# The third stage of a fused transformer decoder block: its fp32 products as three products of rounded parts, one input loaded transposed, mask rows sent with the fills

## The chip, the cores and the metric

The kernel runs as one program on 1 core of one Trainium2 chip. The metric is device time of the whole program in microseconds (us). Three runs of the kernel before gave 4870.12, 4870.19 and 4873.30 us, median 4870.19 us.

## The reference, cut to what matters

Input `x` is 128 x 128 x 256 (batch, channel, length), `ctx` has the same shape. Four stages follow each other:

```
x1  = LN(attn_conv(q=x, k=v=ctx, causal mask) + x)          # 8 heads, grouped conv of width 3 as projection
o1  = LN(x1 + mha1(x1, x1, x1, mask1))                      # 16 heads of depth 16, d_model 256
o2  = LN(o1 + mha2(v=ctx, k=ctx, q=o1, mask2 per batch))    # queries from o1, keys and values from ctx
out = LN(o2 + relu(o2 @ w1 + b1) @ w2 + b2)

def _mha(v, k, q, mask, wq, bq, wk, bk, wv, bv, wo, bo):
    qh = split(q @ wq + bq); kh = split(k @ wk + bk); vh = split(v @ wv + bv)
    logits = einsum('bhqd,bhkd->bhqk', qh, kh) / sqrt(16) + mask * -1e9
    return einsum('bhqk,bhkd->bhqd', softmax(logits), vh) @ wo + bo
```

The change is about the third stage (`mha2`).

## The kernel before, in words

`build` runs `constants`, then `attention` three times (`phase` 0, 1, 2), then `feed_forward`. A pass of `attention` works on units of 512 tokens; phases 1 and 2 have 32 units of 4 tiles of 128 tokens. The text calls phase 2 the third stage and phase 1 the second.

A unit has 16 slots. `PLANS[phase]` says by hand in which slot each engine does which step, and each engine's program is written out from it (`body(t)`); nothing is scheduled at run time, so a late step holds up all that stands behind it on its engine. Attention of unit t takes slots 0 to 15: in each slot `attend_step` (scores, turned, with the row maxima subtracted) on TensorE, `exp_step` on ScalarE, and after every fourth one `pv_tile` (probabilities times values). In the same slots other units are at other steps: the projections of unit t+2 (`project_step`), the values of unit t+1, the scores of unit t+1 that only serve the row maxima (`score_step`, with `max_of` on VectorE), the output product, residual, moments and normalisation of the tiles just attended.

Where the operands come from matters here. Queries and keys are split into three bf16 parts (`HI`, `MID`, `LO`), and SyncE's queue then copies them with 12 DMAs per half unit (`fill_stack`) into `stack`, from which scores are made: 96 rows of parts, 3 rows of the mask of the batch (`mask_parts`) and 3 rows of maxima. The SP queue has one order: in each unit `fill_mask(t+1)`, `fill_stack(t+1, 1)`, `load(t+3)`, `store(t-1)`, `load_resid(t+1)`, `fill_stack(t+2, 0)`. `fill_mask` therefore stands behind the 12 DMAs of `fill_stack(.., 0)`. The first score of unit t+1 (slot 4) waits for it.

In the third stage all products with weights are plain fp32 products. `ctx` arrives with tokens on partitions, so `context_step` turns it on TensorE (2 steps of 4 transposes a unit) and `context_out` copies it to `cin` on ScalarE. The second stage does the same products in another way: operands are split into two rounded parts of type F32R and multiplied three times (`PRODUCTS`: high x high, high x low, low x high). There ScalarE rounds the input (`round_x`), and GpSimd takes the rest (`rest_of_x`).

Of the kernel before, what the change touches and what calls it, by code (L numbers as in the profile page):

```python
# [22 lines left out]
F32 = mybir.dt.float32  # L23
# [73 lines left out]
        dve_steps={'recip': (5, 2), 'merge': (6, 0), 'add': (8, 1), 'stats': (8, 2), 'moments': (8, 2), 'epsilon': (8, 2)},  # L97
        pe_masks=(),
        split_lag=0,
        work=[((0,), 'context', 2, 0),  # L100
              ((0, 1), 'values', 1, 0),
              ((3,), 'values', 1, 1),
              ((3,), 'turn_y', -1, 2),
              ((5,), 'max', 0, 1),
              ((5, 6), 'project', 2, 0),
              ((7,), 'project', 2, 1),
              ((7,), 'context', 2, 1),
              ((9,), 'project', 2, 2),
              ((10,), 'turn_y', -1, 3),
              ((11,), 'project', 2, 3),  # L110
              ((12,), 'max', 1, 0),
              ((14,), 'turn_y', 0, 0),
              ((15,), 'turn_y', 0, 1)],
    ),
# [118 lines left out]
def constants(nc, top, l0, io, c):  # L233

    def sb(name, shape, dt=F32):
        c[name] = top.enter_context(nc.sbuf_tensor(name, shape, dt))
        return c[name]

    def sb_l0(name, shape, dt=F32):
# [10 lines left out]
    mask1 = sb("mask1", [P, P])  # L250
    mask1t = sb("mask1t", [P, P])
    rows = {n: sb(n, [P, L]) for n in ("ln1_g", "ln1_b", "ln2_g", "ln2_b", "ln3_g", "ln3_b",
                                       "mha1_bo", "mha2_bo", "ffn_b2")}
# [7 lines left out]
    c["weights"] = {m: {n: sb(f"{m}_{n}", [P, 2, L]) for n in ("wq", "wk", "wv", "wo")} for m in ("mha1", "mha2")}  # L261
    c["weights_in"] = top.enter_context(nc.semaphore("weights_in"))
# [133 lines left out]
def attention(nc, top, c, io, phase):  # L396
# [32 lines left out]
    with ExitStack() as ctx:  # L429
# [10 lines left out]
        if conv:  # L440
            x_pad = sb("x_pad", [P, 2, BU, L + 2])
            c_pad = sb("c_pad", [P, 2, BU, L + 2])
        else:
            xin = sb("xin", [P, 2, 2, TOK])
        if phase == 2:
            craw = sb("craw", [P, 2, TILES, L])
            cin = sb("cin", [P, 2, 2, TOK])
        if phase == 0:
            x_parts = [sb(f"{n}_parts", [P, 2, 2, BU, L + 2], F32R) for n in ("x", "c")]
        elif phase == 1:  # L450
            x_rounded = sb("x_rounded", [P, 2, 2, TOK], F32R)
        if not conv:
            wq, wk, wv, wo = (c["weights"][name][n] for n in ("wq", "wk", "wv", "wo"))

        w_split = [] if phase == 2 else [(w, sb(f"w{n}_parts", [P, 2, w.shape[1], w.shape[2]], F32R))
# [1071 lines left out]
```

## Time and profile before

| | |
|---|---|
| median of three runs | 4870.19 us |
| the profiled execution, its own time | 4873.18 us |
| its span (first to last instruction) | 4871.4 us |
| mean granted TensorE clock | 0.970 |
| busy over the span: PE, DVE, ACT, POOL | 90%, 72%, 64%, 58% |
| first and last load of the residual in the third stage | at 2955.9 and 4071.9 us |

PE is TensorE, PEld its weight loads, DVE VectorE, ACT ScalarE, POOL GpSimd, SP the queue of SyncE. Busy shares over the span are means over four stages. What a change in one stage is worth has to be read from the rows of that stage. All times of rows are us from the start of the span, unless ns is written.

### The profile page before, as it was taken

To read this page: it belongs to the slowest core of one execution; us is meant where nothing else is said; L and a number is where in the kernel's file an instruction comes from. 1 tells how busy PE (TensorE), PEld (TensorE's weight loads), DVE (VectorE), ACT (ScalarE), POOL (GpSimd) and SP (SyncE) were. 2 spreads that over 40 slices of the span, in tenths; PEclk is the share of its full clock that TensorE was granted. 3 is DMA by queue.
4 is the path that set the end of the run, shared out by engine and by line. 5 is a ranking of instruction groups with operands and counts; after the bars stand their busy time and mean duration, and the time that the engine had idled before them with its cause. 6 is when DMAs were issued, how large, how long until landed. Compare 5 with 4: busy or idle time off the path is not lost. (4 is left out here: it accounts for less than half of the span.)

```text
span 4871.4 us, 150045 instructions
## 1 busy us (share of the span) xinstructions
PE 4403.9 (90%) x46221; PEld 3437.6 (71%) x46221; DVE 3528.8 (72%) x14161; ACT 3110.8 (64%) x6280; POOL 2832.4 (58%) x4362
## 2 busy tenths in 40 slices
PE   5999999999999958999999967899999996999999
PEld 4777677677777647777777755666666664899998
DVE  4888888888888848888888864555555554666665
ACT  3777777777777747777777754566566664544443
POOL 2655655655656536777777744556565563455555
PEclk8999999999999979999999988999999998999999
DMA  4333333333333325555555534555555553222221
GB/s 100 114 112 113 109 113 109 111 114 108 111 116 107 106 75 157 155 158 165 152 155 164 153 101 140 157 169 162 164 164 162 167 166 111 74 65 77 65 69 56
DMA packets 1047398, 602.17 MB, mean 124 GB/s; under 512 B 64057, under 2 KB 1047017, under 8 KB 1047273
## 3 DMA queue, kind: packets, MB, share of 16 engines
q1 hardware_dynamic: 1037288, 595.97, 42.7%
q10 hardware_dynamic: 9984, 4.72, 0.3%
q8 instruction: 56, 0.92, 0.1%
q14 instruction: 70, 0.57, 0.0%
HBM read 175.86 MB, written 117.54 MB: 60 GB/s over the span
## 5 line engine op out<-in xcount | busy, mean ns | idle before, releaser
L1049 DVE CUSTOM_DVE_ANT_0 l_junk<-l_bank,mask 128x256 bf16<-128x256 f32 x2048 | 775.9, 419 | 126.5 <-PE l_bank L782 104.6
L940 ACT ACTIVATE mha_probs<-mha_bank 128x512 f32<-128x512 f32 x1024 | 607.8, 601 | 330.2 <-PE mha_bank L812 179.7
L940 ACT ACTIVATE l_probs<-l_bank 128x512 f32<-128x512 f32 x1024 | 612.1, 598 | 232.5 <-DVE l_bank L1064 170.7
L1064 DVE TENSOR_TENSOR l_bank<-l_bank,mask0t 128x512 f32<-128x512 f32 x640 | 445.4, 696 | 103.1 <-PE l_bank L812 92.2
L1049 DVE CUSTOM_DVE_ANT_0 mha_junk<-mha_bank,mask 128x128 bf16<-128x128 f32 x2048 | 466.4, 284 | 64.7 <-PE mha_bank L782 61.1
L1040 DVE TENSOR_REDUCE mha_max_parts<-mha_bank 128x4 f32<-128x512 f32 x512 | 331.4, 683 | 217.6 <-PE mha_bank L782 214.2
L782 PE MATMUL mha_bank<-mha_stack 96*128 96x128 bf16 (+1 forms) x4096 | 363.7, 222 | 121.2 <-DMA mha_stack<-mask_parts 41.0
L812 PE MATMUL mha_bank<-mha_stack 99*128 99x128 bf16 (+1 forms) x4096 | 407.5, 222 | 55.9 <-DMA mha_stack<-mha_max_rows 52.2
L782 PE MATMUL l_bank<-l_stack 96*128 96x256 bf16 x2048 | 369.4, 276 | 71.6 <-DVE l_max_parts L1049 56.6
L812 PEld LDWEIGHTS mha_bank<-mha_stack 99*128 99x128 bf16 (+1 forms) x4096 | 305.5, 99 | 174.0 <-issue 54.9
L812 PE MATMUL l_bank<-l_stack 99*128 99x128 bf16 x4096 | 405.1, 221 | 13.6 <-issue 5.3
L1169 POOL TENSOR_TENSOR mha_yproj<-mha_yproj,mha_parts 128x512 f32<-128x512 f32 x256 | 296.7, 1159 | 200.9 <-ACT mha_parts L913 200.8
L1366 ACT ACTIVATE ffn_hidden<-ffn_h,ffn_b_s 128x512 f32<-128x512 f32 x256 | 176.8, 691 | 354.8 <-PE ffn_h L1320 336.4
L812 PEld LDWEIGHTS l_bank<-l_stack 99*128 99x128 bf16 x4096 | 256.1, 99 | 207.0 <-issue 177.7
L1064 DVE TENSOR_TENSOR mha_bank<-mha_bank,mask1t 128x512 f32<-128x512 f32 x512 | 354.8, 693 | 59.9 <-PE mha_bank L812 57.9
L1320 PE MATMUL ffn_h<-ffn_x_parts,ffn_w_parts 128*128 128x512 f32 x1536 | 373.8, 393 | 21.4 <-DVE ffn_x_parts L1381 20.8
L1333 PEld LDWEIGHTS ffn_o<-ffn_w_parts,ffn_hidden_parts 128*128 128x128 f32 x3072 | 384.9, 191 | 11.6 <-issue 2.0
L1333 PE MATMUL ffn_o<-ffn_w_parts,ffn_hidden_parts 128*128 128x256 f32 x3072 | 388.2, 283 | 1.6 <-DVE ffn_hidden_parts L1386 1.6
L782 PEld LDWEIGHTS mha_bank<-mha_stack 96*128 96x128 bf16 (+1 forms) x4096 | 253.6, 98 | 185.6 <-issue 99.6
L1386 DVE TENSOR_TENSOR ffn_hidden_parts<-ffn_hidden,ffn_hidden_parts 128x512 fp32r<-128x512 f32 x256 | 246.4, 963 | 181.5 <-ACT ffn_hidden_parts L1366 180.4
L1320 PEld LDWEIGHTS ffn_h<-ffn_x_parts,ffn_w_parts 128*128 128x128 f32 x1536 | 281.7, 189 | 75.6 <-issue 21.1
L1175 POOL TENSOR_TENSOR mha_parts<-mha_yproj,mha_parts 128x512 bf16<-128x512 f32 x256 | 296.7, 1159 | 59.3 <-ACT mha_parts L977 56.4
(176 smaller groups left out, 11473.5 us busy)
## 6 DMA issues: line engine op xcount, KB each, us to landing
mha_stack<-mha_parts SPq DMA_DIRECT2D x1536, 128.0 KB, 2.4
l_stack<-l_parts SPq DMA_DIRECT2D x1024, 64.0 KB, 2.0
l_stack<-l_parts SPq DMA_DIRECT2D x256, 128.0 KB, 2.3
rows_o<-mha_y SPq DMA_DIRECT2D x64, 512.0 KB, 3.8
cols_o<-mha_y_t SPq DMA_DIRECT2D x128, 256.0 KB, 2.8
l_x_pad<-in_x SPq DMA_DIRECT2D x64, 256.0 KB, 2.8
l_c_pad<-in_ctx SPq DMA_DIRECT2D x64, 256.0 KB, 3.0
l_resid<-in_x SPq DMA_DIRECT2D x64, 256.0 KB, 2.7
```

What stands on the lines that cost most here:

```text
L782: mm = nc.tensor.matmul(sbank[i % 2][:, s * KEYS:(s + 1) * KEYS], stack[0:SCORED, u.par, place(0, h), j * P:(j + 1) * P], stack[0:SCORED, ...
L812: mm = nc.tensor.matmul(tbank[i % 2][:, s * P:(s + 1) * P], stack[0:STACKED, u.par, place(1, h), key:key + P], stack[0:STACKED, u.par, pla ...
L940: nc.scalar.activation(probs[:, i % RING, :], tbank[i % 2][:, :], ACT.Exp).then_inc(att_exp, 1)
L1040: nc.vector.tensor_reduce(max_parts[:, j, 0, col:col + SH * GROUPS - 1:GROUPS], sbank[i % 2][:, :].rearrange("p (s k) -> p s k", s=SH), op ...
L1049: ins = nc.vector.tensor_tensor_reduce(out=junk[:, i % 2, cols], in0=sbank[i % 2][:, cols], in1=mask, scale=1.0, scalar=LOWEST, op0=ALU.ad ...
L1064: nc.vector.tensor_tensor(bank_, bank_, mask.unsqueeze(1).to_broadcast([P, 4, P]), ALU.add).then_inc(att_masked, 1)
L1169: nc.gpsimd.tensor_tensor(rest, rest, parts[:, u.par, i, HI, :], ALU.subtract).then_inc(rest_step, 1)
L1175: nc.gpsimd.tensor_tensor(parts[:, u.par, i, LO, :], rest, parts[:, u.par, i, MID, :], ALU.subtract).then_inc(split_done, 1)
L1320: mm = nc.tensor.matmul(hbank[f % 4][:, :], w1_parts[:, a, kt, f * P:(f + 1) * P], x_parts[:, u.par, b, kt, :], start=(i == 0), stop=(i == 5))
L1333: mm = nc.tensor.matmul(obank[j][:, 0:L], hidden_parts[:, u.par, b, f, j * P:(j + 1) * P], w2_parts[:, a, f, :], start=(f == 0 and i == 0) ...
L1366: last = nc.scalar.activation(out, hbank[f % 4][:, :], ACT.Relu, bias=c["ffn_b1_s"][:, f:f + 1])
L1386: nc.vector.tensor_tensor(hidden_parts[:, u.par, 1, f, :], hidden[:, f % 2, :], hidden_parts[:, u.par, 0, f, :], ALU.subtract).then_inc(h_ ...
```

## The change: what it does

Third stage:

- `ctx` is also given transposed (`ctx_t`), and is loaded by two DMAs of 256 KB straight into `cin`, as `xin` is. `context_step`, `context_out` and the buffer `craw` are gone.
- `xin` and `cin` have one buffer each in place of two. `load(u)` waits until both were split for the unit before (`x_lo`, `c_lo`).
- All products with weights become three F32R products. For that ScalarE rounds `xin` and `cin` (`round_x`, two instructions of 128x1024, in slot 13, for unit t+3), GpSimd takes the rest of `xin` (`rest_of_x`), VectorE the rest of `cin` (`rest_of_c`, new). `merged_out` writes a rounded `merged_t`, and VectorE takes its rest (`merged_low`, new, four a unit). The weights are split at the head of the stage.
- The mask rows go in two halves, each in `fill_stack` ahead of the wait for `split_done`.
- The plan has new slots.

Other stages: the weights of `mha1` are loaded at the head of the first stage and split there, those of `mha2` in the next units; `y` of the third stage lies in the buffer of its raw weights (`carried`). Loops of the first two stages and of the feed-forward are as they were.

```diff
-        score=[4, 4, 6, 7, 8, 8, 9, 9, 11, 11, 12, 12, 13, 14, 15, 17],
+        score=[4, 5, 7, 7, 8, 9, 9, 10, 11, 12, 12, 14, 16, 16, 18, 19],
-        steps={'turn': 6, 'turn_merged': 7, 'output': 8, 'normalise': 9},
+        steps={'turn': 5, 'turn_merged': 7, 'output': 8, 'normalise': 9},
...
+        split_slot=13,
...
             def load(u):
-                if exists(u.plus(-2), N):
+                if phase == 2:
+                    wait_sp(sp, x_lo, u.u, passed["sp"])
+                    wait_sp(sp, c_lo, u.u, passed["sp"])
+                elif exists(u.plus(-2), N):
...
-            def fill_mask(u):
-                wait_sp(sp, att_mm, CHUNKS * (u.u - 1) if u.number() not in (0, 1) else 0, passed["sp"])
-                sp.dma_start(stack[STACK:SCORED, u.par, side_of((1,)), :],
-                             mask2_units[u.u].unsqueeze(1).to_broadcast([3, H, TOK])).then_inc(mask_in[u.par], 16)
...
+                if phase == 2:
+                    sp.dma_start(stack[STACK:SCORED, u.par, side_of((1,)), tokens],
+                                 mask2_units[u.u][:, tokens].unsqueeze(1).to_broadcast([3, H, 2 * P])
+                                 ).then_inc(stack_in[u.par][half], 16)
                 wait_sp(sp, split_done, projected(u, HALVES - 1), passed["sp"])
...
             def output_step(u, j):
+                if phase == 2:
+                    pe.wait_ge(mt_low, TILES * u.u + j + 1)
+                    for kt in range(2):
+                        for a, b in PRODUCTS:
+                            mm = nc.tensor.matmul(fbank[:, 0:L], merged_t_parts[:, b, kt, :], w_parts[3][:, a, kt, :],
...
+            def rest_of_c(u):
+                dve.wait_ge(x_hi, u.u + 1)
+                nc.vector.tensor_tensor(x_part(1, u.par, 1), raw(1, u.par), x_part(1, u.par, 0), ALU.subtract
+                                        ).then_inc(c_lo, 1)
+
+            def merged_low(u, j):
+                dve.wait_ge(mt_out, TILES * u.u + j + 1)
+                nc.vector.tensor_tensor(merged_t_parts[:, 1, :, :], fbank[:, 0:2 * P].rearrange("p (a s) -> p a s", a=2),
+                                        merged_t_parts[:, 0, :, :], ALU.subtract).then_inc(mt_low, 1)
...
+                        if slot == SPLIT_SLOT and exists(t.plus(3), N):
+                            rest_of_c(t.plus(3))
```

How the instructions stand now, at three places. First TensorE in the third stage, where one unit ends and the next begins. `mha_craw` is `ctx` as loaded, `mha_z` the sum to be normalised, `mha_probs` the probabilities. Before:

```order
L860 MATMUL mha_bank<-ident,mha_z 128x128 x2
L848 MATMUL mha_bank<-ident,mha_merged 128x128 x2
L799 ISA
L812 MATMUL mha_bank<-mha_stack 128x128 x4
L822 REGISTER_ALU
L826 MATMUL mha_bank<-mha_probs,mha_vals 17x128 x16
L145 REGISTER_ALU
L716 MATMUL mha_bank<-ident,mha_craw 128x128 x4
L145 REGISTER_ALU
L765 MATMUL mha_bank<-mha_wv,mha_cin 128x256 x2
L854 MATMUL mha_bank<-mha_wo,mha_merged_t 128x256 x2
```

The same place now; L868 was L860, L849 L848, L813 L812, L827 L826, L783 is the score product (L782), and L857 the output product (L854).

```order
L868 MATMUL mha_bank<-ident,mha_z 128x128 x2
L849 MATMUL mha_bank<-ident,mha_merged 128x128 x2
L800 ISA
L813 MATMUL mha_bank<-mha_stack 128x128 x4
L823 REGISTER_ALU
L827 MATMUL mha_bank<-mha_probs,mha_vals 17x128 x16
L144 REGISTER_ALU
L783 MATMUL mha_bank<-mha_stack 128x128 x4
L144 REGISTER_ALU
L783 MATMUL mha_bank<-mha_stack 128x128 x4
L857 MATMUL mha_bank<-mha_w_parts,mha_merged_t_parts 128x256 x6
```

The four transposes of `ctx` are gone, the values have moved behind this place, two score steps have come in, and the output product has 6 instructions in place of 2.

Second, ScalarE in slots 12 to 14 of the third stage, now (L943 is the exponential, L931 and L933 the row maxima and their DMA, L978 `round_x`):

```order
L948 ACTIVATE mha_heads_out<-mha_bank 128x512
L940 REGISTER_ALU
L943 ACTIVATE mha_probs<-mha_bank 128x512
L1009 REGISTER_ALU
L931 ACTIVATE mha_max_rows<-mha_bank 48x256
L933 DMA mha_stack<-mha_max_rows 3x16x256
L972 ISA
L978 ACTIVATE mha_x_pair<-mha_xin 128x1024
L978 ACTIVATE mha_c_pair<-mha_cin 128x1024
L940 REGISTER_ALU
L943 ACTIVATE mha_probs<-mha_bank 128x512
```

Before, the same stretch (with the maxima a slot earlier) had nothing between the DMA and the next exponential:

```order
L945 ACTIVATE mha_heads_out<-mha_bank 128x512
L1003 REGISTER_ALU
L928 ACTIVATE mha_max_rows<-mha_bank 48x256
L930 DMA mha_stack<-mha_max_rows 3x16x256
L937 REGISTER_ALU
L940 ACTIVATE mha_probs<-mha_bank 128x512
L937 REGISTER_ALU
L940 ACTIVATE mha_probs<-mha_bank 128x512
```

Two instructions of 128x1024 have come between two exponentials.

Third, the SP queue at the head of the third stage's loop. Before, where `fill_mask` is L638 and `fill_stack` L656:

```order
L163 ISA
L638 ISA
L638 DMA mha_stack<-mask_parts 3x16x512
L150 ISA x2
L656 DMA mha_stack<-mha_parts 16x16x256 x12
L150 ISA
L621 ISA
L621 DMA mha_xin<-cols_o 128x4x128
```

And now, up to the second input:

```order
L673 ISA
L673 DMA mha_stack<-mask_parts 3x16x256
L149 ISA
L678 DMA mha_stack<-mha_parts 16x16x256 x12
L149 ISA
L646 ISA
L646 DMA mha_xin<-cols_o 128x4x128
L646 ISA
L646 DMA mha_xin<-cols_o 128x4x128
L646 DMA mha_cin<-in_ctx_t 128x4x128 x2
```

What stands here is the second half of a unit's fills, with the second half of its mask; the first half of the mask now stands in the same way ahead of the other 12, at the end of the body of the unit before.

## Rows read from the trace of the kernel before

**Rows 1.** Windows: 25 units of the third stage (busy us by engine).
```profile
3076.00:3968.40 892.40, 815.98 (x8704) 609.55 (x8700) 512.59 (x1201) 551.08 (x1151) 513.97 (x626) 0.98 0.58 164
```

**Rows 2.** Source L646, a move for each of 26 loads: durations, first and last start.
```profile
L646 SPq MOVE mha_resid<-rows_x x26: 29/29/29, 1919.2 to 2757.6; - x26
L646 SPq MOVE mha_resid<-rows_o x26: 29/38/38, 3076.0 to 3968.5; - x26
```

**Rows 3.** Waits in 3076.0 to 3968.4 us: us in total, times, longest.
```profile
PE mha_bank L782 <- DMA mha_stack<-mask_parts: 34.8, 21, 2.8
```

**Rows 4.** Timeline of PE in the third stage: start us, us, engine, line.
```profile
3410.03 1.95 PE L765 MATMUL mha_bank<-mha_wv,mha_cin 128*128 128x256 f32 x8
3411.81 0.38 PE L860 MATMUL mha_bank<-ident,mha_z 128*128 128x128 f32 x2
...
3415.42 0.62 PE L782 MATMUL mha_bank<-mha_stack 99*128 99x128 bf16 x8 [1.79 <-DMA mha_stack<-mask_parts]
...
3422.13 1.94 PE L742 MATMUL mha_bank<-mha_xin,mha_wq 128*128 128x512 f32 x4
3423.91 0.60 PE L716 MATMUL mha_bank<-ident,mha_craw 128*128 128x128 f32 x4
3424.34 0.38 PE L848 MATMUL mha_bank<-ident,mha_merged 128*128 128x128 f32 x2
...
3426.34 1.08 PE L854 MATMUL mha_bank<-mha_wo,mha_merged_t 128*128 128x256 f32 x4
3427.26 0.39 PE L812 MATMUL mha_bank<-mha_stack 102*128 102x128 bf16 x4
...
3429.78 0.39 PE L812 MATMUL mha_bank<-mha_stack 102*128 102x128 bf16 x4
3430.00 0.39 PE L860 MATMUL mha_bank<-ident,mha_z 128*128 128x128 f32 x2
3430.23 0.60 PE L839 MATMUL mha_bank<-ident,mha_heads_out 128*128 128x128 f32 x4
3430.66 0.39 PE L812 MATMUL mha_bank<-mha_stack 102*128 102x128 bf16 x4
```

**Rows 5.** Timeline of PE in the second stage: one value tile, then one projection.
```profile
2708.23 0.39 PE L759 MATMUL mha_bank<-mha_w_parts,mha_x_rounded 128*128 128x256 f32 x1
...
2709.05 0.40 PE L812 MATMUL mha_bank<-mha_stack 99*128 99x128 bf16 x4
...
2711.15 0.47 PE L739 MATMUL mha_bank<-mha_x_rounded,mha_w_parts 128*128 128x512 f32 x1
...
2712.59 0.38 PE L860 MATMUL mha_bank<-ident,mha_z 128*128 128x128 f32 x2
```

**Rows 6.** Timeline of the SP queue in the third stage.
```profile
3403.11 7.91 SPq L656 DMA_DIRECT2D mha_stack<-mha_parts  x12
3411.95 0.29 SPq L638 DMA_DIRECT2D mha_stack<-mask_parts  x1
```

**Rows 7.** Windows: the stretch behind the wait at 3415 us.
```profile
3417.20:3419.80 2.60, 2.60 (x9) 1.17 (x8) 1.24 (x5) 0.86 (x2) 0.55 (x1) 0.51 0.72 200
```

**Rows 8.** Timeline of ACT in the third stage.
```profile
3435.99 0.38 ACT L928 ACTIVATE mha_max_rows<-mha_bank 48x256 bf16<-48x256 bf16 x1
3436.40 0.73 ACTq L930 DMA_DIRECT2D mha_stack<-mha_max_rows  x1
3437.25 1.09 ACT L940 ACTIVATE mha_probs<-mha_bank 128x512 f32<-128x512 f32 x2 [0.88 <-PE mha_bank L812]
```

**Rows 9.** Sources L972 and L1381: ns min/median/max, first and last start us.
```profile
L972 ACT ACTIVATE mha_x_rounded<-mha_xin x32: 1041/1077/1081, 1773.2 to 2797.0; 128x1024 fp32r<-128x1024 f32 x32
L1381 DVE TENSOR_TENSOR ffn_x_parts<-ffn_xin,ffn_x_parts x32: 1217/1219/3442, 4138.3 to 4811.0; 128x1024 fp32r<-128x1024 f32 x32
```

**Rows 10.** Timelines of POOL and DVE in the feed-forward stage.
```profile
4307.45 2.41 POOL L1444 TENSOR_TENSOR ffn_resid<-ffn_resid,ffn_b 128x1024 f32<-128x1024 f32 x1
4307.98 2.43 DVE L1386 TENSOR_TENSOR ffn_hidden_parts<-ffn_hidden,ffn_hidden_parts 128x512 fp32r<-128x512 f32 x1 [2.12 <-ACT ffn_hidden_parts L1366]
```

More of the change, by code:

```diff
@@ L462, in x_part @@
                 return x_parts[n][:, par, part, :, :]
-            return xin[:, par, :, :].bitcast(F32R) if part else x_rounded[:, par, :, :]
+            if phase == 1:
+                return xin[:, par, :, :].bitcast(F32R) if part else x_rounded[:, par, :, :]
+            return c_pair[:, par, part, :, :] if n else x_pair[:, part, :, :]
         resid = sb("resid", [P, 2, TILES * W])
@@ L495, in attention @@
         resid_ld = [sem(f"resid_ld{i}") for i in range(2)]
-        mask_in = [sem(f"mask_in{i}") for i in range(2)]
         padded = sem("padded")
@@ L542, in attention @@
                   if not (conv and pair[0] == pair[1])]
+        FILLED = len(FILLS) + (1 if phase == 2 else 0)
         def place(side, h):
@@ L676, in body @@
             def body(t):
-                if phase == 2 and exists(t.plus(1), N):
-                    fill_mask(t.plus(1))
                 if exists(t.plus(1), N):
@@ L880, in body @@
                             value_step(u, step, bank_, piece, pieces)
-                        elif what == "context":
-                            context_step(u, step, bank_)
                         elif what == "max":
@@ L968, in round_x @@
                     act.wait_ge(xin_ld[u.par], 16 * XIN_LOADS * (u.k + 1))
-                if exists(u.plus(-2), N):
-                    act.wait_ge(work_mm, work_count(u.plus(-2), "values", VSTEPS - 1))
-                for n, x in enumerate(raw):
-                    last = nc.scalar.activation(x_part(n, u.par, 0), x[:, u.par, :, :], ACT.Copy)
+                readers = [(u.plus(-1), "project", GROUPS - 1)] if phase == 2 and exists(u.plus(-1), N) else []
+                readers += [(u.plus(-2), "values", VSTEPS - 1)] if exists(u.plus(-2), N) else []
+                if readers:
+                    act.wait_ge(work_mm, work_count(*max(readers, key=lambda at: banks.at[at[1:]][0])))
+                for n in range(INPUTS):
+                    last = nc.scalar.activation(x_part(n, u.par, 0), raw(n, u.par), ACT.Copy)
                 last.then_inc(x_hi, 1)
@@ L1138, in body @@
                             mid_part(t.plus(2), P_SLOT.index(slot - 1))
-            iterations(nc, dve, N, 2, 1, body)
+                        if slot == SPLIT_SLOT and exists(t.plus(3), N):
+                            rest_of_c(t.plus(3))
+                if conv and t.number() == -1:
+                    for n, parts_ in enumerate(c["mha1_parts"]):
+                        dve.wait_ge(c["next_w_hi"], n + 1)
+                        nc.vector.tensor_tensor(parts_[:, 1, :, :], c["weights"]["mha1"][n], parts_[:, 0, :, :],
+                                                ALU.subtract).then_inc(c["next_w_lo"], 1)
+            iterations(nc, dve, N, 3 if phase == 2 else 2, 1, body)
         @block.gpsimd
@@ L1230, in body @@
                         pad_edges(t.plus(3))
-                    if slot == SPLIT_SLOT and phase != 2 and exists(t.plus(3), N):
+                    if slot == SPLIT_SLOT and exists(t.plus(3), N):
                         rest_of_x(t.plus(3))
```

207 lines of the change are left out of this document (104 added, 103 removed).

## The prediction

> **What bounds the kernel now.** I first took the period of a unit in each stage. Loads of the residual come once a unit, and 26 of them span 892.4 us in the third stage, so a unit takes 35.70 us there; in the second stage it takes 838.4 / 25 = 33.54 us [rows 2]. That is odd, since the second stage does the same products and more work on VectorE. Then I read the windows of the third stage: TensorE is busy 815.98 of 892.4 us (91%), ScalarE 62%, VectorE and GpSimd 57 and 58% [rows 1]. TensorE bounds the stage, with 76.4 us idle, 3.06 us a unit. Of these the mask rows take 34.8 us, 1.39 us a unit [rows 3]. The SP queue shows why: the mask's DMA is issued at 3411.95, behind 12 fills that began at 3403.11, and TensorE stands until 3415.42 [rows 4, 6]. The other 1.67 us a unit are small waits. Behind the long wait the granted clock is 0.51 for a while, which is the lower level (1.2 GHz) [rows 7]; over the stage it is 0.98 [rows 1].
>
> **The work of TensorE, step by step.** Products of fp32 are priced from the third stage, products of rounded parts from the second, start to next start, all at the full clock.
> - Projections, 4 steps a unit. Now 3422.13 to 3423.91 = 1.78 us [rows 4]; as six F32R products 2711.15 to 2712.59 = 1.44 us [rows 5]. Saved 4 x 0.34 = 1.36.
> - Values, 4 tiles a unit. Two tiles now take 3410.03 to 3411.81 = 1.78, one 0.89 [rows 4]; as six products 2708.23 to 2709.05 = 0.82 [rows 5]. Saved 4 x 0.07 = 0.28.
> - Output product, 4 a unit. Now 3426.34 to 3427.26 = 0.92 [rows 4]; afterwards six products of the very shape of a value tile, 0.82. Saved 4 x 0.10 = 0.40.
> - Transposes of `ctx`, 2 steps a unit: 3423.91 to 3424.34 = 0.43 each [rows 4]. Saved 0.86.
>
> Together 2.90 us a unit, for 32 units 93 us. All of it lies on the engine that bounds the stage. I see no reason why it should be less than zero or more than 3.3 (the same with 0.05 more for each of the eight 256-column tiles).
>
> **The waits of TensorE.** The mask's 1.39 us go: its halves are now issued before the wait for the last split, well ahead of the fills. What is late next at slot 4 is the 12 fills themselves. The mask was issued at 3411.95 and released TensorE at 3415.42, 3.5 us later; the last of the 12 fills was issued at about 3410.4 (one takes 7.91 / 12 = 0.66), so by the same delay it was there at about 3413.9. TensorE arrived at 3415.42 - 1.79 = 3413.6 [rows 4, 6]. So fills and TensorE arrive together today, and a TensorE that does the same slots 1.6 us sooner (context, two output products, the values and a part of the waits) would wait up to 1.9 us for fills. That would eat the gain from the mask, unless something else holds TensorE up between slot 12 and slot 4. Something does:
>
> ScalarE gets two rounding instructions of 128x1024 in slot 13. One takes 1.04 us [rows 9]. In the order they stand behind the row maxima and their DMA, ahead of exponential 14, and TensorE may not start chunk 0 of the next unit before exponential 14 is done. From the end of chunk 13 on TensorE: exponential 13 about 0.65 with its start, maxima 0.41 (3435.99 to 3436.40), DMA issue 0.85 (to 3437.25) [rows 8], two roundings 2.08 [rows 9], exponential 14 about 0.5 (two take 1.09 [rows 8]). Sum 4.49. TensorE itself has there: maxima turned and `turn_heads` 0.22 + 0.43, chunk and score 14 0.22 + 0.23, chunk 15 0.22, two `turn_y` and one `turn_merged` 3 x 0.22, together 1.98 (each from the four rows from 3429.78 on and from 3424.34 [rows 4]; I take 0.22 for all 2-matmul steps). New wait: 2.5 us. Then values of chunk 15 wait for exponential 15, about 0.2. ScalarE's `context_out` is gone, but in slots where it wasn't on this path; it counts as nothing.
>
> VectorE gets `rest_of_c`, again 128x1024: alone 1.22 us [rows 9]. It starts when the rounding ends, so it ends 0.6 us after exponential 14 if undisturbed, and score 13 and the output product of tile 2 need the maximum and `merged_low` behind it. Undisturbed this adds nothing. But GpSimd's rest of `xin` and its affine steps read SBUF at the same time. In the feed-forward stage such a subtraction of half the size took 2.43 us, ending 0.55 us after a GpSimd addition of 2.41 us that had begun 0.53 us before it [rows 10]: it did nothing until GpSimd was through. So `rest_of_c` costs 1.22 us at best, and 2.41 + 1.22 = 3.6 at worst for one collision. I take 1.9, nearer to the lower end: in my chain GpSimd is in the second affine instruction of tile 1 when `rest_of_c` becomes ready, the long rest of `xin` stands behind that, and in rows 10 VectorE got its turn as soon as one GpSimd instruction ended. This adds 0.5 us to the wait at the output product. `merged_low` (four a unit, reads PSUM and one operand in SBUF) lies beside a `pv_tile` and costs nothing; if VectorE is late, it carries the delay over, which is counted.
>
> The Trainium skill (SBUF — State Buffer, Who interferes with whom) states the rule behind this: a VectorE instruction with two SBUF inputs and a GpSimd instruction that reads SBUF exclude each other, whichever starts first keeps the port pair to its end. By that rule, the two rests, both released by the same rounding, cannot overlap at all; the row agrees (2.43 us). It is what the second rival is made of.
>
> New waits: 2.5 + 0.2 + 0.5 = 3.2 us a unit, where there were 3.06. With TensorE 3.2 us late in slot 0 it is no longer early at slot 4, so the fills cost nothing. The other waits of 1.67 us I count as gone: two of them sat between slots 13 and 15, inside the stretch that ScalarE now sets. Bounds: 0.5 (ScalarE ready sooner, as there is slack of one exponential) plus 1.9 for the fills, against 5.7 if `rest_of_c` takes 3.6. Net I take +0.14 a unit, +4 us in 32 units. The clock: a stretch with 3.2 us of waits is as likely to be followed by the low level as the present one; I keep 0.98 and count nothing. Bound: 2% of 35.7 is 0.7 us a unit if it never falls.
>
> **Loads.** With one buffer, `load(t+3)` is issued after both sets of 12 fills: from the first fill 2 x 8.2 (7.91 and a mask of 0.29 [rows 6]), then four issues of about 0.5, so 18.4 us, and needs some 3 us to land. The rounding is a unit later, 31 us after the first fill. Hidden with 9 us to spare.
>
> **The ends.** At the head of the third stage ScalarE rounds four weights (each 512 columns, half of 1.04, so 2.1 us together, beside the input's DMA), then both inputs 2.1, then GpSimd 2.4 [rows 9, 10] before the first projection, which before waited for DMAs alone. That is about +3 us. In the first stage four more DMA issues stand between the first fills, and three weights are split in line ahead of unit 0: +3 us. The second stage starts without splitting, but its first product waits for the input's split anyway: 0. Together +6 us, between 0 and +12.
>
> **Sum.** -93 + 4 + 6 = -83 us against the profiled execution's own 4873.18 us (span 4871.4), so 4790. That execution is 3.0 us above the median, so against the median of 4870.19 it gives 4787 us. I correct nothing else. The unit comes out at 35.70 - 2.90 + 0.14 = 32.9 us.
>
> **Rivals.** All are for the median.
> 1. *The waits dissolve.* ScalarE runs ahead enough for the two roundings, because exponential 13 and the maxima come sooner than in my chain; then the fills set slot 4, at 1.9 us a unit, and the clock falls less (0.5 us a unit gained). Unit: 35.70 - 2.90 - 3.06 + 1.9 + 0.5 of other waits - 0.5 = 31.6; -130 + 6: 4746 us. For it: VectorE and GpSimd have over 40% idle, ScalarE 38% [rows 1]. Against: ScalarE is strictly in order there.
> 2. *The lock, once.* The rest of `xin` starts first on GpSimd, and `rest_of_c` takes 3.6 us, not 1.9: +1.7 a unit, 54 us, 4841 us. For it: both are released by the same rounding. Against: GpSimd is in its affine steps when that comes.
> 3. *Slower: the lock, twice.* GpSimd goes from the rest of `xin` straight on to the bias of the residual, also 128x1024 (2.41 us [rows 10]), without VectorE getting in. `rest_of_c` then ends 2.4 us later still, score 13, the output product and the normalisation behind it too: +2.4 x 32 = 77 on the second rival, 4918 us. The place is VectorE in slots 14 to 0; it decides once `rest_of_c` ends more than 2.6 us a unit later than forecast (83 / 32). Against: in rows 10 VectorE gets the port as soon as one GpSimd instruction ends.
> 4. *It is no faster product for product*: the six products change the loaded operand more often, and only the transposes are gained: -28 (32 x 0.86) + 4 + 6, 4852 us. Against: rows 5 are just these products in such company.
>
> **How the numbers follow.** Forecast (4770 to 4810) 0.50; first rival 0.24; second 0.13; third 0.06; fourth 0.07. A measurement of this kernel can tell 0.2% (10 us) from no change, thus 4860 and 4880 are the borders. Faster: all of the forecast and first rival, 0.11 of the second, 0.04 of the fourth, 0.89. Same: 0.02 + 0.03 = 0.05. Slower 0.06. The range leaves out the lower third of the first rival (0.08) and the third, with parts of the second and fourth above it: 4728 to 4852.
>
> **What the changed profile would show.** Right: a period of 32 to 33.5 us between residual loads in the third stage; no wait of the score product for `mask_parts`; a wait of TensorE's chunk 0 for `mha_probs` of ScalarE of about 2 us a unit, with `round_x` running ahead of it; projection steps of 1.44 us there; `rest_of_c` between 1.2 and 2.5 us in the mean. First rival: waits for DMA `mha_stack<-mha_parts` at the first score and a period under 32. Second and third: `rest_of_c` at 3.6 us or more and a score product or output product that waits for VectorE. My chain would be wrong if TensorE's waits lie in other slots than 13 to 0, for there I found none.

## The result, and the profile after

The kernel after took 4720.83 us (median of four runs, 4716.57 to 4722.3); beside it the kernel before took 4871.74 us (4870.12 to 4883.3). The ratio is 0.9684, 95% interval 0.9667 to 0.9701: 3.2% faster. I had forecast 4787 us in a range of 4728 to 4852. The direction was right, the gain was nearly twice the forecast, and the time lies just below the range. The profiled execution took 4722.3 us (span 4720.5 us), 150.9 us less than the profiled one before.

The windows view of the third stage after, for 25 units again (columns as in [rows 1]: stretch, its length, busy us of PE, PEld, DVE, ACT and POOL, granted clock, DMA share, GB/s), and the source of the residual's load, that gives the period:

```profile
3065.40:3832.10 766.70, 714.62 (x9083) 609.68 (x9072) 610.66 (x1323) 577.16 (x1147) 596.35 (x648) 1.00 0.66 191
```

```profile
L664 SPq DMA_DIRECT2D mha_resid<-rows_o x32: 394/507/1135, 2966.4 to 3928.1; - x32
L664 SPq MOVE mha_resid<-rows_x x26: 29/34/38, 1923.7 to 2762.4; - x26
L664 SPq MOVE mha_resid<-rows_o x26: 29/29/29, 3065.4 to 3832.2; - x26
```

A unit takes (3832.2 - 3065.4) / 25 = 30.67 us in place of 35.70 [rows 1, 2], 5.03 us less. The second stage stands where it stood: 838.7 / 25 = 33.55 us. TensorE's idle time is (766.7 - 714.6) / 25 = 2.08 us a unit in place of 3.06, and the granted clock 1.00 in place of 0.98 [rows 1]. The 150.9 us come from three places: from the first to the last load of the stage it is 961.7 us in place of 1116.0 (-154.3); the first load comes 10.5 us later, at 2966.4; and from the last load to the end it is 7.1 us less.

The waits of TensorE in that window (waited for, us in total, times, longest):

```profile
PE mha_bank L868 <- DVE mha_z L1095: 37.4, 25, 1.5
PE mha_bank L840 <- DVE mha_z L1124: 6.7, 25, 0.3
PE mha_bank L813 <- ACT mha_probs L943: 6.4, 24, 0.3
```

The mask is gone from the list [rows 3], and so is every DMA: the fills didn't take its place. What is left sits between chunk 13 of one unit and chunk 0 of the next (chunk n is the attention step of slot n), as forecast, but the greater part stands under the normalised `z`, which `turn_y` (L868) turns; L840 is `turn_heads`. TensorE's timeline there (start us, us, engine, line; idle before it in brackets):

```profile
3376.43 0.40 PE L813 MATMUL mha_bank<-mha_stack 102*128 102x128 bf16 x4
...
3377.34 0.63 PE L840 MATMUL mha_bank<-ident,mha_heads_out 128*128 128x128 f32 x4 [0.29 <-DVE mha_z L1124]
...
3378.48 0.39 PE L868 MATMUL mha_bank<-ident,mha_z 128*128 128x128 f32 x2
3380.36 0.41 PE L868 MATMUL mha_bank<-ident,mha_z 128*128 128x128 f32 x2 [1.50 <-DVE mha_z L1095]
3380.61 0.38 PE L849 MATMUL mha_bank<-ident,mha_merged 128*128 128x128 f32 x2
3381.28 0.38 PE L813 MATMUL mha_bank<-mha_stack 102*128 102x128 bf16 x4 [0.29 <-ACT mha_probs L943]
...
3390.36 0.40 PE L783 MATMUL mha_bank<-mha_stack 99*128 99x128 bf16 x4
...
3390.91 0.96 PE L857 MATMUL mha_bank<-mha_w_parts,mha_merged_t_parts 128*128 128x256 f32 x6
3391.72 0.40 PE L813 MATMUL mha_bank<-mha_stack 102*128 102x128 bf16 x4
...
3395.01 1.62 PE L750 MATMUL mha_bank<-mha_x_pair,mha_w_parts 128*128 128x512 f32 x6
3396.46 0.38 PE L849 MATMUL mha_bank<-ident,mha_merged 128*128 128x128 f32 x2
```

The fp32 rows of [rows 4] have these for an answer: a projection is 3396.46 - 3395.01 = 1.45 us (forecast 1.44), an output product 3391.72 - 3390.91 = 0.81 (forecast 0.82). L783 is the score product of slot 4, the first that needs the fills. The queue of SyncE issued them here:

```profile
3380.16 7.91 SPq L678 DMA_DIRECT2D mha_stack<-mha_parts  x12
```

The last of the 12 was issued at about 3387.4 (3380.16 + 11 x 0.66), and the score product began 3.0 us later without a wait.

ScalarE's timeline beside it shows the chain I had worked out, in its order: exponential 13, maxima, their DMA, two roundings, exponentials 14 and 15.

```profile
3376.86 0.60 ACT L943 ACTIVATE mha_probs<-mha_bank 128x512 f32<-128x512 f32 x1 [0.45 <-PE mha_bank L813]
3377.36 0.36 ACT L931 ACTIVATE mha_max_rows<-mha_bank 48x256 bf16<-48x256 bf16 x1
3377.75 0.73 ACTq L933 DMA_DIRECT2D mha_stack<-mha_max_rows  x1
3378.64 1.06 ACT L978 ACTIVATE mha_x_pair<-mha_xin 128x1024 fp32r<-128x1024 f32 x1 [0.93 <-ACT mha_max_rows L931]
3379.61 1.04 ACT L978 ACTIVATE mha_c_pair<-mha_cin 128x1024 fp32r<-128x1024 f32 x1
3380.55 1.06 ACT L943 ACTIVATE mha_probs<-mha_bank 128x512 f32<-128x512 f32 x2
```

VectorE, then GpSimd, in the same stretch:

```profile
3379.08 1.14 DVE L1095 TENSOR_SCALAR mha_z<-mha_z,mha_moments,mha_rstd 128x256 f32<-128x256 f32 x1
3380.68 1.44 DVE L1041 TENSOR_TENSOR mha_c_pair<-mha_cin,mha_c_pair 128x1024 fp32r<-128x1024 f32 x1 [0.46 <-ACT mha_c_pair L978]
```

```profile
3378.92 1.15 POOL L1202 TENSOR_TENSOR mha_parts<-mha_yproj,mha_parts 128x512 bf16<-128x512 f32 x1
3380.30 0.74 POOL L1236 TENSOR_TENSOR carried<-mha_z,ln_g 128x256 f32<-128x256 f32 x1 [0.23 <-DVE mha_z L1095]
3381.12 1.59 POOL L1238 TENSOR_TENSOR carried<-carried,ln_b 128x256 f32<-128x256 f32 x1
```

The sources of two VectorE lines (ns min/median/max, first and last start):

```profile
L1041 DVE TENSOR_TENSOR mha_c_pair<-mha_cin,mha_c_pair x32: 1220/1404/1670, 2927.1 to 3875.5; 128x1024 fp32r<-128x1024 f32 x32
```

```profile
L1095 DVE TENSOR_SCALAR mha_z<-mha_z,mha_moments,mha_rstd x128: 402/414/1366, 2998.0 to 3967.6; 128x256 f32<-128x256 f32 x128
```

`rest_of_c` takes 1.40 us in the median, not the 1.9 I took, and no score or output product is in the list of waits behind it. It is GpSimd that loses here: its L1238 began 0.44 us after `rest_of_c` and took 1.59 us, where its like (L1236) takes 0.74. One line higher VectorE lost: the normalisation (0.41 us in the median) began 0.16 us after GpSimd's L1202 and took 1.14, to 0.15 us after L1202 had ended. The Trainium skill (SBUF — State Buffer, Who interferes with whom) states both cases: the engine that comes second stands still until the other's instruction is through, and besides a two-input subtraction a `tensor_scalar` can take the shared ports too. By that rule, the trace agrees in both that the second engine is held (1.59 and 1.14 us). By the recorded times it does not show a full standstill: the held instructions ended 0.59 and 0.15 us after the other had ended, less than the 0.74 and 0.41 us that they take alone.

### The profile page after: what moved, and what is told of

It reads as the page before. It is cut to its first block and busy times, and to the rows that moved or that the text cites. A ratio compares the mean times of both kernels' runs of the same rounds, so it can differ in the third digit from the quotient of the medians.

```text
span 4720.5 us, 151301 instructions
## 1 busy us (share of the span) xinstructions
PE 4284.9 (91%) x46733; PEld 3450.4 (73%) x46733; DVE 3659.4 (78%) x14325; ACT 3147.0 (67%) x6284; POOL 2939.8 (62%) x4394
## 5 line engine op out<-in xcount | busy, mean ns | idle before, releaser
L943 ACT ACTIVATE mha_probs<-mha_bank 128x512 f32<-128x512 f32 x1024 | 606.7, 600 | 252.4 <-DVE mha_bank L1084 146.0
L943 ACT ACTIVATE l_probs<-l_bank 128x512 f32<-128x512 f32 x1024 | 611.5, 597 | 234.0 <-DVE l_bank L1084 174.6
L813 PE MATMUL mha_bank<-mha_stack 99*128 99x128 bf16 (+1 forms) x4096 | 407.9, 223 | 61.0 <-DMA mha_stack<-mha_max_rows 53.9
L783 PE MATMUL l_bank<-l_stack 96*128 96x256 bf16 x2048 | 369.4, 276 | 70.7 <-DVE l_max_parts L1069 56.6
L783 PE MATMUL mha_bank<-mha_stack 96*128 96x128 bf16 (+1 forms) x4096 | 370.8, 222 | 54.2 <-DMA mha_stack<-mha_parts 37.0
L813 PE MATMUL l_bank<-l_stack 99*128 99x128 bf16 x4096 | 405.8, 221 | 14.7 <-issue 6.5
L813 PEld LDWEIGHTS l_bank<-l_stack 99*128 99x128 bf16 x4096 | 256.5, 99 | 210.1 <-issue 181.2
L813 PEld LDWEIGHTS mha_bank<-mha_stack 99*128 99x128 bf16 (+1 forms) x4096 | 287.1, 99 | 133.7 <-DMA mha_stack<-mha_max_rows 38.0
L783 PEld LDWEIGHTS mha_bank<-mha_stack 96*128 96x128 bf16 (+1 forms) x4096 | 255.3, 99 | 117.8 <-issue 46.7
L1202 POOL TENSOR_TENSOR mha_parts<-mha_yproj,mha_parts 128x512 bf16<-128x512 f32 x256 | 297.8, 1163 | 58.8 <-ACT mha_parts L983 56.5
```

The costliest lines, as they stand in the source:

```text
L783: mm = nc.tensor.matmul(sbank[i % 2][:, s * KEYS:(s + 1) * KEYS], stack[0:SCORED, u.par, place(0, h), j * P:(j + 1) * P], stack[0:SCORED, ...
L813: mm = nc.tensor.matmul(tbank[i % 2][:, s * P:(s + 1) * P], stack[0:STACKED, u.par, place(1, h), key:key + P], stack[0:STACKED, u.par, pla ...
L943: nc.scalar.activation(probs[:, i % RING, :], tbank[i % 2][:, :], ACT.Exp).then_inc(att_exp, 1)
L1202: nc.gpsimd.tensor_tensor(parts[:, u.par, i, LO, :], rest, parts[:, u.par, i, MID, :], ALU.subtract).then_inc(split_done, 1)
```

## The experiments

After the result, what was open: how much the mask gave by itself; whether the waits of 2.1 us are one chain or two that end together; what the products gave; and where 0.7 us a unit had come from that neither waits nor product durations account for. The last is the clock. Over the 25 units, the stretches at the lower level (1.2 GHz) add up to 44.4 us before and 6.8 us after. My estimate is that a low stretch costs half its length where TensorE has work, by the two levels of 1.2 and 2.4 GHz; so this is worth (44.4 - 6.8) / 25 / 2 = 0.75 us a unit.

For each kernel the same reading was made. "Low" is the time at the lower level, and the last column is the median against the kernel before, measured beside it.

| kernel | unit us | idle us | low us | median us | ratio (95%) |
|---|---|---|---|---|---|
| before | 35.70 | 3.06 | 1.77 | 4871.74 | |
| after | 30.67 | 2.08 | 0.27 | 4720.83 | 0.9684 (0.9667 to 0.9701) |
| after_again | 30.68 | 2.11 | 0.41 | 4720.66 | 0.9682 (0.9666 to 0.9698) |
| a_mask_halves_only | 34.10 | 1.68 | 1.50 | 4824.10 | 0.9887 (0.9871 to 0.9904) |
| b_mask_late | 32.75 | 2.81 | 3.14 | 4792.01 | 0.9828 (0.9807 to 0.9849) |
| c_act_extra | 32.70 | 3.14 | 2.73 | 4778.21 | 0.9791 (0.9774 to 0.9807) |
| d_fp32_output | 32.06 | 2.07 | 2.73 | 4749.63 | 0.9733 (0.9717 to 0.9750) |
| e_turn_y_later | 31.00 | 2.37 | 0.41 | 4732.11 | 0.9703 (0.9687 to 0.9719) |
| f_turn_y_later_round_15 | 31.60 | 2.91 | 0.27 | 4756.00 | 0.9750 (0.9734 to 0.9767) |
| i_slots_of_before | 33.08 | 2.93 | 2.73 | 4788.58 | 0.9818 (0.9802 to 0.9835) |
| k_one_more_transposition | 31.38 | 2.05 | 1.37 | 4740.79 | 0.9716 (0.9699 to 0.9733) |
| l_four_more_transpositions | 31.45 | 1.95 | 0.96 | 4746.44 | 0.9734 (0.9718 to 0.9750) |

The change of idle time and half the change of low time don't always sum to the change of the unit: in the experiments below about 0.3 us a unit can be left, either way. Terms smaller than that are not shown by this count.

**The mask alone, in the kernel before.** Nothing else of the change is in it.

```diff
+                if phase == 2:
+                    sp.dma_start(stack[STACK:SCORED, u.par, side_of((1,)), tokens],
+                                 mask2_units[u.u][:, tokens]...).then_inc(stack_in[u.par][half], 16)
                 wait_sp(sp, split_done, projected(u, HALVES - 1), passed["sp"])
...
-                if phase == 2 and exists(t.plus(1), N):
-                    fill_mask(t.plus(1))
```

> The kernel before with one part of the change: the mask rows in halves, each ahead of its fills. Theory 1 (the wait for the mask and the low clock behind it are a large part of the gain): the wait of 1.4 to 1.5 us a unit goes and slow clock falls from 44 us to under 15 us in 25 units, 0.6 us a unit; 32 x 2.0 = 64 us less, about 4806 us. Rival (as in the prediction: fills arrive with TensorE, and the clock does not depend on this wait): fills take over 0.3 us or more of the wait, the clock stays, 30 to 45 us less, 4825 to 4840 us.

The unit fell by 1.60 us, the time to 0.9887. Its windows and its waits:

```profile
3066.60:3919.10 852.50, 810.48 (x8708) 608.25 (x8704) 512.01 (x1201) 551.45 (x1152) 514.64 (x626) 0.98 0.60 172
```

```profile
PE mha_bank L779 <- DVE mha_max_parts L1037: 19.6, 25, 0.8
PE mha_bank L857 <- DVE mha_z L1072: 19.3, 25, 0.8
PE mha_bank L809 <- issue: 2.7, 12, 0.2
PE mha_bank L779 <- DMA mha_stack<-mha_parts: 0.4, 1, 0.4
```

The wait for the fills is 0.4 us in 25 units. With the mask's 34.8 us away, nothing took their place. The 1.9 us for fills that I had given the first rival doesn't appear.

The time, 55 us less, lies between what the two theories gave (64, and 30 to 45). The clock half of mine failed: low time fell to 37.5 us in 25 units and not to under 15. The clock records show where it went. Of the 13 low stretches before, 7 begin within 2 us behind the end of a wait for the mask, the other 6 at the small waits at the end of a unit. Without the mask's wait all 11 begin there, 6.4 to 7.0 us behind the load of the residual. They come regularly, each 68.2 or 68.3 us after the last, which is two units of 34.10.

**The mask late, in the kernel after.** The whole mask goes back behind 12 fills; all else stays.

```diff
-                if phase == 2:
-                    sp.dma_start(stack[STACK:SCORED, u.par, side_of((1,)), tokens], ...)
...
+                if phase == 2 and exists(t.plus(1), N):
+                    fill_mask(t.plus(1))
```

> The changed kernel with the mask rows as one transfer behind the 12 fills of the first half, as before. Issued at about 3388.4 in the period that was read, it would land 3.5 us later, at 3391.9, where TensorE arrives at 3390.4. Theory 1: 1.5 us a unit of wait and 0.6 us of low clock, +67 us, about 4788 us. Rival (the waits in slots 13 to 0 give the time back, and the clock holds): under +25 us.

```profile
PE mha_bank L874 <- DVE mha_z L1101: 37.5, 25, 1.5
PE mha_bank L789 <- DMA mha_stack<-mask_parts: 20.0, 19, 2.4
PE mha_bank L846 <- DVE mha_z L1130: 6.8, 25, 0.3
PE mha_bank L819 <- ACT mha_probs L949: 4.3, 16, 0.3
```

The wait for the mask came back with 20.0 us, 0.80 us a unit. The unit grew by 2.08: 0.73 of idle and (3.14 - 0.27) / 2 = 1.43 of low clock, which is 0.08 too much. So in the changed kernel the late mask costs more by the clock than by itself. But the low clock doesn't stand behind the mask's wait: of the 23 low stretches 4 begin there, and 19 at the 1.50 us wait for `z`, which the kernel after has as well with 2 low stretches in all. The time came out near the 4788 us that I expected, with half the wait (0.80 for 1.5) and twice the clock (1.43 for 0.6), so the number was luck.

**More work for ScalarE in slot 13.** Ahead of each of the two roundings stands one pass of 128x512 into a buffer that nothing reads. If ScalarE's chain has slack under the wait for `z`, some of it vanishes.

```diff
+                    if phase == 2:
+                        wait(act, extra_done, 2 * u.u + n)
+                        nc.scalar.activation(extra[:, :], raw(n, u.par)[:, 0, :], ACT.Copy).then_inc(extra_done, 1)
```

> The changed kernel with two more instructions of 128x512 on ScalarE among the roundings of slot 13 (0.5 to 0.6 us each, results unused). Theory 2 (ScalarE's in-order chain from exponential 13 to exponential 14 sets chunk 0 of the next unit, with at most 0.3 us of slack): +0.8 to 1.1 us a unit, +26 to 35 us, about 4750 us. Rival (the normalisation on VectorE, held by the port that it shares with GpSimd, sets that stretch, and ScalarE has slack): under +10 us.

```profile
PE mha_bank L870 <- DVE mha_z L1100: 37.5, 25, 1.5
PE mha_bank L815 <- ACT mha_probs L945: 32.5, 25, 1.4
PE mha_bank L842 <- DVE mha_z L1129: 7.0, 25, 0.3
```

The wait for `mha_probs` rose from 6.4 to 32.5 us, 1.04 us a unit, which is what two such passes take (0.52 to 0.53 us each, from start to start). ScalarE's chain has no slack. The low clock took up to 1.23 us a unit on top; with the 1.06 of idle that is 0.26 more than the 2.03 by which the unit grew. I had expected about 4750 us, and the clock is what I had left out.

**The output product as fp32.** `merged_low` and the six products of L857 give way to two fp32 products with a copy of the weights.

```diff
-                        for a, b in PRODUCTS:
-                            mm = nc.tensor.matmul(fbank[:, 0:L], merged_t_parts[:, b, kt, :], w_parts[3][:, a, kt, :], ...
+                for kt in range(2):
+                    mm = nc.tensor.matmul(fbank[:, 0:L], merged_t[:, kt, :], wo[:, kt, :], ...
```

> The changed kernel with the output product of the third stage back in plain fp32 (two products in place of six, no merged_low on VectorE). Theory 3 (the six products are worth their start-to-start difference, 0.92 against 0.80 us, four a unit): +15 us, about 4736 us. Rival (merged_low on a VectorE that is 80% busy costs as much as the products save): within 5 us of 4721 us, or below.

```profile
3061.50:3863.10 801.60, 749.77 (x8876) 624.79 (x8868) 575.94 (x1222) 577.78 (x1147) 594.90 (x648) 0.96 0.64 183
```

The idle time is that of the kernel after (2.07 against 2.08 us), and yet a unit takes 1.39 us more. Four output products, from start to start 0.92 us each and not 0.80, should give 0.48. Low clock gives (2.73 - 0.27) / 2 = 1.23, which leaves 0.16 of the 1.39 for them; so the product step by itself is worth between 0.16 and 0.48 us a unit, and I can't say it closer. I had expected 15 us more, and it is 29. It is the clock that makes this kernel slower, and at the same idle time: it doesn't follow the sum of the waits.

**The second `turn_y` a slot later.** If the wait for `z` alone set the end of the unit, moving its reader behind chunk 0 would save up to 1.5 us a unit. If ScalarE's chain ends at the same time, it saves nothing.

```diff
-        work=[((1, 2), 'values', 1, 0),
+        work=[((0,), 'turn_y', -1, 1),
+              ((1, 2), 'values', 1, 0),
...
-              ((15,), 'turn_y', 0, 1)],
```

> The changed kernel with the turn of tile 1's normalised rows (turn_y) moved from slot 15 to slot 0 of the next unit, so that TensorE does not wait there for VectorE's normalisation (1.50 us a unit). Theory 2 (ScalarE's chain exponential 13, maxima, two roundings, exponential 14 is as late as the normalisation): the wait moves to chunk 0 of the next unit (for mha_probs), the sum of both falls by 0.3 us a unit at most, the time stays within 10 us of the base. Rival (the normalisation alone set it): 1.2 us a unit or more, 38 us less.

```profile
PE mha_bank L813 <- ACT mha_probs L943: 40.0, 25, 1.6
PE mha_bank L849 <- DVE mha_merged L1109: 8.9, 25, 0.4
```

TensorE from chunk 13 to chunk 0 of the next unit:

```profile
3133.83 0.40 PE L813 MATMUL mha_bank<-mha_stack 102*128 102x128 bf16 x4
...
3138.68 0.38 PE L813 MATMUL mha_bank<-mha_stack 102*128 102x128 bf16 x4 [1.63 <-ACT mha_probs L943]
```

The wait for `z` is gone and the wait for `mha_probs` has gone from 6.4 to 40.0 us. From chunk 13 to chunk 0 it is 3138.68 - 3133.83 = 4.85 us, the very time of the kernel after. The unit is 0.33 us longer, and the kernel 11 us slower, where I had expected it within 10. Two chains end together: in the kernel after, ScalarE's was forecast and hidden behind the other one's name in the list.

**That, and the roundings in slot 15.** This takes the roundings out of ScalarE's chain too.

```diff
-        split_slot=13,
+        split_slot=15,
```

> As the kernel before it, and the roundings in slot 15 in place of 13, where TensorE has the product with the values, two scores and an output product ahead of the next exponential that it needs. Theory 2: both chains are gone, 1.5 to 2 us a unit of waits less; then TensorE comes to slot 4 early and waits there for the fills, up to 0.5 us on the trace read (fills at about 3390.3, arrival 3390.4 less 2); net 0 to 1 us a unit, 0 to 30 us less. Rival (GpSimd is then late with the rest of the input, the bias and the reciprocal root of tile 2): new waits of turn_y in slot 3, no gain or a loss of 30 us.

```profile
PE mha_bank L840 <- DVE mha_z L1124: 44.5, 49, 1.6
PE mha_bank L813 <- DMA mha_stack<-mha_max_rows: 14.4, 25, 2.5
PE mha_bank L868 <- DVE mha_z L1095: 4.5, 24, 0.2
```

Both waits went (0.18 us a unit is left of the one for `z`), and others came, so that idle time is 0.8 us more: `turn_heads` for the residual's addition, and chunks for the maxima's DMA. I had named neither of these. The kernel is 35 us slower than the kernel after beside it. Slot 13 is the better of the two places.

**The kernel after again**, as a base for the two experiments before it and the next.

> The changed kernel once more, as the base of this call. 4716 to 4722 us on the chip of the first runs; low clock 0.1 to 0.4 us a unit and a period of 30.67 us if its clock is a trait of the kernel; 1 us of low clock or more and some 30 us more time if it was chance.

4720.66 us against 4720.83, a unit of 30.68 against 30.67 us: even the low clock repeats (0.41 and 0.27, three stretches and two).

**The slots of before, in the kernel after.** The other tables of the plan go back in the same way, and the roundings stay in slot 13.

```diff
-        score=[4, 5, 7, 7, 8, 9, 9, 10, 11, 12, 12, 14, 16, 16, 18, 19],
+        score=[4, 4, 6, 7, 8, 8, 9, 9, 11, 11, 12, 12, 13, 14, 15, 17],
-        steps={'turn': 5, 'turn_merged': 7, 'output': 8, 'normalise': 9},
+        steps={'turn': 6, 'turn_merged': 7, 'output': 8, 'normalise': 9},
```

> The changed kernel with the slots of the plan before (without the two context steps; merged_low in slot 7, roundings in slot 13). Everything else of the change stays. Theory 4 (products, mask and loads carry the gain, the slots little): recorded waits 1.5 to 3 us a unit, +0 to 30 us. Rival (the new slots are what makes room for roundings and merged_low): waits over 3.5 us a unit, +50 us or more.

```profile
3069.50:3896.40 826.90, 753.55 (x9104) 630.19 (x9100) 575.63 (x1324) 578.69 (x1151) 595.75 (x650) 0.96 0.62 178
```

It takes 68 us more than the kernel after beside it, where my theory had 0 to 30. A unit has 2.41 us more: 0.85 of idle, 1.23 of low clock, and about 0.3 that I can't place. The new slots are thus worth nearly half of the whole gain, half of this again by the clock. Taken off one at a time, the early mask (2.08 us a unit) and the slots (2.41) with the products' own time (about 3.0, below) make more than the 5.03 of the whole, so the parts don't add up: the old slots have a price of their own once the roundings stand in slot 13.

**One transposition more, and four.** These ask what brings the low clock back: fp32 output products as in the experiment above, or a longer unit. The line stands in the output step of the third stage, in its first tile alone (`j == 0`), or in all four:

```diff
+                if phase == 2 and j == 0:
+                    for a in range(2):
+                        mm = nc.tensor.transpose(fbank[:, a * P:(a + 1) * P], merged[:, a * P:(a + 1) * P], c["ident"][:, :])
```

> One transposition pair of merged more per unit of the third stage, its result overwritten at once (about 0.22 us of TensorE each time, by the 0.43 us that a group of four such matmuls takes between starts). What is open is what brings the 3.4 us stretches at 1.2 GHz back: d_fp32_output had the same waits as after (2.07 against 2.08 us a unit) and 2.73 us a unit at the low clock against 0.27. Theory A, it follows what TensorE computes at the time (d's four-byte products themselves): the clock here stays as in after (about 0.3 to 0.4 us a unit low), period 30.7 + 0.2 = 30.9 us, time 4720.8 + 25 x 0.22 = 4726 us. Theory B, it follows how long the unit is (d's period of 30.8 before the low clock came on top): some low stretches return here, 1 to 2.7 us a unit, which is 0.5 to 1.2 us of period, time 4740 to 4755 us.

> The same with four pairs per unit, one in each output slot: about 0.88 us of TensorE more per unit and no wait added. Theory A (the clock follows the four-byte products of d): 0.3 to 0.4 us a unit at the low clock, period 30.7 + 0.9 = 31.6 us, time 4721 + 22 = 4743 us. Theory B (it follows the length of a unit): about 2.7 us a unit low, as in d and in the kernels with the slots of before, period 31.6 + 1.2 = 32.8 us, time about 4773 us. Where the added work is partly hidden by the waits of 2.1 us a unit (the wait for the normalisation in the output slot's second product is 1.5 us), the waits fall by what it covers and the period grows by less than 0.9.

Neither theory holds for both. The first run came out as theory B had it (1.37 us low, 4740.79 us). The second is near theory A in time (4746.44 us for 4743), though not in low clock (0.96 us for 0.3 to 0.4). One added pair brought the low time from 0.27 to 1.37 us a unit and lengthened the unit by 0.71 us: 0.55 by the clock, the rest its own work. With the output products as in the kernel after, this isn't a matter of fp32 output products. But four pairs brought less (0.96 us) in a unit of the same length, and the unit of 31.60 us above had 0.27: it isn't the length of a unit either. The windows of the first of the two, in two units on end: for each the stretch of the wait, begun 0.2 us into it, and the stretch behind that:

```profile
3105.20:3108.60 3.40, 1.73 (x36) 1.35 (x40) 2.88 (x4) 3.40 (x7) 3.09 (x3) 1.00 0.24 66
3108.70:3112.00 3.30, 3.30 (x31) 2.81 (x20) 2.22 (x5) 1.79 (x5) 3.30 (x3) 0.50 0.66 183
3137.50:3140.90 3.40, 1.77 (x36) 1.43 (x40) 2.93 (x4) 3.40 (x7) 3.09 (x3) 1.00 0.24 65
3140.90:3144.30 3.40, 3.40 (x47) 3.06 (x40) 3.01 (x9) 2.43 (x6) 3.40 (x3) 1.00 0.71 198
```

The two first stretches are alike in everything, with the same wait:

```profile
3106.52 0.41 PE L871 MATMUL mha_bank<-ident,mha_z 128*128 128x128 f32 x2 [1.50 <-DVE mha_z L1098]
...
3138.82 0.41 PE L871 MATMUL mha_bank<-ident,mha_z 128*128 128x128 f32 x2 [1.50 <-DVE mha_z L1098]
```

Once the clock fell behind it (0.50) and once it didn't (1.00). So what TensorE did in the wait's own stretch doesn't choose the units. The choice is not without order either: in this trace the low stretches of the 25 units, past the first, begin by turns 61.4 and 95.6 us apart (to 0.1 us), two and three units. What makes this order is open; no run varied it by itself.

## Why the prediction was wrong, step by step

**The products** were the soundest term. Forecast 2.90 us a unit; by starts, in medians of the steps at the full clock over 25 units, the projections gave 1.18 (forecast 1.36), the values 0.50 (0.28), the output products 0.45 (0.40), and the transposes of `ctx` 0.87 (0.86): together 3.00. The values have more than I read from single places: a tile after takes 0.76 to 0.81 us (forecast 0.82) for 0.89 to 0.92 before. It is within the bound of 3.3, and 0.10 x 32 = 3 us of the miss. The unit's change less idle and clock, 5.03 - 0.98 - 0.75 = 3.30, leaves 0.3 that I can't place.

**"The waits of TensorE", +0.14 a unit.** This step failed: idle time fell by 0.98. The mask went as said, and alone in the kernel before this gave 1.60 us a unit. The chain on ScalarE was right to within 0.2: from chunk 13 (3376.43) to chunk 0 (3381.28) are 4.85 us, forecast 4.49 and a start of 0.22. What failed is how its price was entered. First, 2.5 and 0.2 us are losses from start to start. The measured loss by the same count is 4.85 - 0.22 - 1.98 = 2.65, but I set it against 3.06 us of recorded idle. As recorded idle it is 2.08 (1.50 + 0.29 + 0.29 in the timeline), since the recorded end of a matmul lies behind the point at which the next could begin: the two of 3380.61 take 0.22 us to the next start elsewhere, but end on record at 3380.99, and idle time counts from there. The two readings differ by about 0.5 us a unit, and one stood on each side of my subtraction. Second, 0.5 us for `rest_of_c` behind GpSimd was wrong: it took 1.40 us, and GpSimd stood back. The two make 1.1 us a unit, some 36 us over 32 units, which is this step's miss.

**The clock, counted at nothing.** This step failed too: it gave 0.75 us a unit, 24 us. I had argued that 3.2 us of waits would be followed by the low level as often as before. That was an argument from an amount, and the experiments show amount to be the wrong measure: at 2.08 us of idle there are 0.27 us of low clock, at 2.07 (fp32 output products) 2.73, at 2.91 (the roundings in slot 15) 0.27. Why the kernel after has so little of it isn't shown: the mask's going alone took 0.27 of the 1.50 us of low time. I had bounded this term by 0.7 us, and then left the bound out of the forecast's own range.

**The loads** were hidden, as said: no wait for a projection's input is in the list. **The ends** cost +10.5 us at the head against +6, and gave back 7.1 us behind the last load, which I had not priced.

**The rivals.** The first was nearest by its number (4746 us, a unit of 31.6) and its mechanism was half right: the small waits and the mask did go and the clock did fall less, but ScalarE didn't run ahead, and the fills never set slot 4. My argument for the fills took the mask's delay of 3.5 us from issue to release as theirs; in the kernel after, the score product began 3.0 us behind the last fill's issue and did not wait. Alone in the kernel before, the mask's removal shows 0.4 us of such waits. The lock (second and third rival) did strike, at the normalisation (1.14 us for 0.41), one instruction ahead of where I looked; there ScalarE's chain covers it, as moving the `turn_y` showed (1.50 us of wait gone, none of it gained). The third, a slower kernel, is refuted with the second: nothing waits behind `rest_of_c`. The fourth is refuted by the timeline (1.45 and 0.81 us).

Of the misses, waits 36 us, clock 24 us and products 3 us make 63 us, less 4 for the head and plus 7 for the tail: 66, where 4790 - 4722.3 = 68 was to be explained. The 0.3 us a unit that I can't place would add 10. From the first to the last load there are 31 units and not 32, which takes some 5 away. These terms were each measured once or twice; that they nearly add up is no proof of each.

## What to carry over

Price a wait and the wait it replaces with the same count, either both from start to start or both as recorded idle: here the mix cost 0.5 us a unit. When a chain is forecast to become the wait, look for it also under another releaser's name; two chains that end together show only one, and moving the reader of that one tells them apart. In a kernel bound by TensorE with short waits each unit, leave room for the granted clock on both sides of the forecast, for here it moved the time by 0.55 and 1.23 us a unit through edits that left the idle time as it was.

## What I had not expected of the hardware

- One pair of 128x128 transpositions more in a unit of 30.67 us (k_one_more_transposition) multiplied the time at 1.2 GHz by five, 0.27 to 1.37 us a unit, with the same waits of 1.50 us. The same wait was followed by a clock of 0.50 in one unit and of 1.00 in the next. TensorE's work in the wait's stretch was the same, and no run here says what tells these units apart.
- Low stretches can come at a regular distance: in a_mask_halves_only all 11 begin 68.2 or 68.3 us apart, two units of 34.10, and in k_one_more_transposition, past the first, by turns 61.4 and 95.6 us, two and three units.
- The low stretches of the kernel after, and of c_act_extra, d_fp32_output, i_slots_of_before and k_one_more_transposition past their first units, begin 6 to 12 us behind the load of the residual, thus in or shortly behind the waits at the end of a unit, and nowhere else. In b_mask_late, with a wait of up to 2.36 us for the mask in 19 of the 25 units, 19 of 23 begin at the first kind too.
- A normalisation of 128x256 on VectorE took 1.14 us in place of 0.41 beside a GpSimd subtraction that had begun 0.16 us sooner, and a GpSimd addition 1.59 us in place of 0.74 beside a VectorE subtraction that had begun 0.44 us sooner: in both the one that came second was held.
